# One expert of a top-k mixture computed densely during the routing, the other seven gathered, and the second product turned around

## The reference, cut to what matters

```python
scores = softmax(xt @ Wr)                 # (4096 tokens, 8 experts)
G, idx = top_k(scores.T, 1024)            # each expert picks 1024 tokens
X_in = xt[idx]
h   = gelu(einsum('ekd,edh->ekh', X_in, W1) + b1[:, None, :])   # 128 -> 512
X_e = einsum('ekh,ehd->ekd', h, W2) + b2[:, None, :]            # 512 -> 128
out = zeros((4096, 128)).at[idx].add(G[..., None] * X_e)
x = x + gb * out                          # gb: one row of 128 per batch of 512 tokens
```

## Time and profile before

| | |
|---|---|
| median of 3 runs | 1061.13 us |
| profiled execution | 1051.98 us, its span 1050.2 us |
| mean granted PE clock | 0.858 |
| busy: PE, DVE, POOL, ACT | 822, 581, 453, 433 us |

### The profile page before, as it was taken

The page is one execution under the profiler, slowest core; times in us unless marked ns, Lnnn a source line. Parts: engine busy times, 40 slices in busy tenths (PEclk is TensorE's granted clock), DMA queues, the critical chain, the costliest instruction groups (busy, mean ns, idle before and its releaser), DMA issues. The chain is left out here.

```text
span 1050.2 us, 16881 instructions
## 1 busy us (share of the span) xinstructions
PE 821.7 (78%) x6185; PEld 432.6 (41%) x6185; DVE 580.8 (55%) x1417; ACT 432.5 (41%) x683; POOL 453.2 (43%) x569
## 2 busy tenths in 40 slices
PE   4579898999999999832328999989624999999884
PEld 3223333333334333221215666657412455555443
DVE  3666676757666674116672343300025688888761
ACT  1004554545454455700003233220164687777651
POOL 7201021422323222340026888886546477774423
PEclk9758999989899998955558999985856899999996
DMA  4220443243231311210002333333210100110100
GB/s 125 55 65 10 104 130 82 78 136 86 49 91 42 93 46 46 65 34 11 1 16 48 42 45 42 45 44 29 23 32 10 33 22 12 32 32 22 32 12 20
DMA packets 69289, 50.94 MB, mean 48 GB/s; under 512 B 20241, under 2 KB 63257, under 8 KB 68634
## 3 DMA queue, kind: packets, MB, share of 16 engines
q1 hardware_dynamic: 57946, 41.23, 15.6%
q0 software_dynamic: 11264, 8.66, 6.2%
HBM read 30.78 MB, written 16.99 MB: 45 GB/s over the span
## 5 line engine op out<-in xcount | busy, mean ns | idle before, releaser
L639 DVE TENSOR_REDUCE MX<-bank 128x1 f32<-128x512 f32 (+3 forms) x352 | 215.7, 638 | 87.9 <-PE bank L389 84.0
L503 ACT ACTIVATE PR<-ps_s 128x1024 f32<-128x1024 f32 x160 | 159.0, 1023 | 153.8 <-PE ps_s L353 88.7
L386 PE MATMUL bank<-K,Q 96*128 96x512 bf16 (+3 forms) x512 | 134.6, 323 | 34.5 <-DVE MX L639 18.0
L1043 POOL DMA_INDIRECT d_acc<-Y,idx x64 | 100.1, 1564 | 34.3 <-issue 18.3
L386 PEld LDWEIGHTS bank<-K,Q 96*128 96x128 bf16 x512 | 44.4, 102 | 154.6 <-DVE MX L639 113.3
L1033 POOL DMA_INDIRECT XG<-d_tab,idx x64 | 61.6, 963 | 89.0 <-DVE idx L1158 70.1
L344 PE MATMUL ps_s<-Q,K 99*128 99x512 bf16 x320 | 97.8, 394 | 1.4 <-DMA Q<-d_m 1.3
L1308 ACT ACTIVATE H<-ps_h,b1T 128x512 f32<-128x512 f32 x64 | 44.0, 687 | 122.7 <-PE ps_h L1244 121.3
L389 PE MATMUL bank<-maskT,identb 128*128 128x128 bf16 (+2 forms) x352 | 91.4, 260 | 0.0
L369 PE MATMUL bank<-PR,VE 128*32 128x512 f32 x640 | 90.1, 636 | 0.2 <-ACT PR L503 0.2
L1179 DVE TENSOR_TENSOR Y<-ps_o,XG 128x512 f32<-128x512 f32 x16 | 11.1, 692 | 130.5 <-PE ps_o L1258 122.9
(11 more groups left out here) (282 smaller groups left out, 1407.8 us busy)
## 6 DMA issues: line engine op xcount, KB each, us to landing
Q<-d_q SPq DMA_DIRECT2D x24, 384.0 KB
d_q<-qs SPq DMA_DIRECT2D x24, 128.0 KB, 2.3
d_y<-ysb SPq DMA_DIRECT2D x128, 18.0 KB
d_tab<-tab SPq DMA_DIRECT2D x8, 272.0 KB, 2.4
X<-L_attn_x SPq DMA_DIRECT2D x8, 256.0 KB, 4.9
w<-L_ffn_W SPq DMA_DIRECT2D x8, 256.0 KB, 3.2
d_acc<-zrow SPq DMA_DIRECT2D x1, 2048.0 KB, 9.4
yt<-d_y SPq DMA_DIRECT2D x8, 256.0 KB, 3.3
```

The lines of the kernel that those rows point to most:

```text
L386: nc.tensor.matmul(ps_mx[G % 2][:, x * w:(x + 1) * w], Q[b % QB][0:KR, h, P * g:P * g + P], K[b % QB][0:KR, 0:w], start=(x == 0), stop=Fal ...
L503: nc.scalar.activation(PR[t % 2][:, 2 * half:2 * half + 2, :], ps_s[half][:, :].rearrange("p (a f) -> p a f", a=2), ACT.Exp, scale=DH ** - ...
L639: nc.vector.tensor_reduce(MX[b % 2][:, c:c + len(hs)], ps_mx[G % 2][:, 0:len(hs) * w].rearrange("p (x w) -> p x w", w=w), AX_X, ALU.max).t ...
L1043: nc.gpsimd.indirect_dma_start(out=g.d_acc, out_offset=bass.IndirectOffsetOnAxis(ap=idx[:, e, k:k + 1], axis=0), in_=Y[e % 2][:, k, :], in ...
```

## The change

Expert 0 is taken out of the gathered ones. Its two products are computed for all 4096 tokens, in four chunks of 1024, from plain loads of `d_tab` (XD, the first two share the buffers Y). The chunks 0 to 2 are cut into 56 steps (`dense(k)`) that stand between the routing products of PE; chunk 3 is iteration 8. ITS lists the eleven iterations; the loop over iterations starts at the fourth. ACT writes a chunk's outputs times gb, features on partitions, to YD. After the loop PE transposes YD (L1291) and DVE adds it to X with the selected scores of expert 0 (gate0, zero where not selected).

The seven others (rx is the expert's number less one) keep gather and scatter. `second` now holds w2 and streams 512 columns of H: 8 products of 512 columns instead of 32 of 128 and 8 for the bias. Its result has features on partitions; ACT adds b2 while it copies it to OT (L1414), and PE transposes it back into the same bank (`outputs_T`, L1284) before DVE multiplies. Four lists are made before the loop instead of two, XG has four buffers instead of three, and POOL gathers three experts ahead. Six load semaphores are joined into one, and the chain semaphores are shared between phases.

```diff
+    ITS = (0, 0, 0, 1, 2, 3, 4, 5, 0, 6, 7)
+    LOOP = 3
+    AHEAD = 4
-        gathers(0)
-        gathers(1)
-        for e in range(NE):
-            if e + 2 < NE:
-                gathers(e + 2)
-            scatters(e)
+        for rx in range(3):
+            gathers(rx)
+        for rx in range(NR):
+            if rx + 3 < NR:
+                gathers(rx + 3)
+            scatters(rx)
...
+        for c in range(len(CHUNK_OF)):
             for h in range(2):
+                dve.wait_ge(oT_ps, 2 * NR + 2 * c + h + 1)
+                for i in range(4):
+                    t = NS * c + 4 * h + i
+                    last = V.scalar_tensor_tensor(g.X[:, t, :], ps_o[h][:, P * i:P * i + P], gate0[:, t:t + 1], g.X[:, t, :],
+                                                  ALU.mult, ALU.add)
...
-                for k in range(4):
-                    for c in range(NC_DI):
-                        last = T_.matmul(ps_o[h][:, P * k:P * k + P], H[h][:, c, P * k:P * k + P], g.w2[:, e, c, :],
-                                         start=(c == 0), stop=False)
-                    last = T_.matmul(ps_o[h][:, P * k:P * k + P], ones[0:1, :], B2[0:1, e, :], start=False, stop=True)
+            last = T_.matmul(ps_o[h][:, :], g.w2[:, ITS[it], c, :], H[h][:, c, :], start=(c == 0), stop=(c == NC_DI - 1))
...
+        for r in range(DIGITS):
+            if r >= 2:
+                dense(2 * r - 4)
+                dense(2 * r - 3)
+            pe.wait_ge(cnt_rdy, r + 1)
+            T_.matmul(ps_r[:, 0:3], group[:, :], cnt[:, :], start=True, stop=True).then_inc(sum_rdy, 1)
...
+        for it in range(LOOP, len(ITS)):
+            e, j = ITS[it], it - LOOP
+            for h in range(2):
+                for c in range(NC_DI):
+                    if ITS[it - 1] and h == 0 and c == 2:
+                        outputs_T(it - 1, 1)
+                    first(it, h, c)
...
+            sp.dma_start(XD[c][:, :, :], g.d_tab[CAP * c:CAP * c + CAP, 0:D].rearrange("(k p) f -> p k f", p=P)
+                         ).then_inc(d_in[c], 16)
```

More of the change, by code:

```diff
@@ L244, in program @@
     lgr = sb0("lgr", [P, NT])
[L247 removed]
+    s_x = [sem("x_loaded0"), sem("x_loaded1"), sem("x_loaded_rest")]
     s_w, s_wqkv, s_wrest = sem("weights_loaded"), sem("qkv_weights_loaded"), sem("other_weights_loaded")
@@ L935, in moe @@
     NG = P // NE
+    NR = NE - 1
+    ITS = (0, 0, 0, 1, 2, 3, 4, 5, 0, 6, 7)
+    CHUNK_OF = {it: c for c, it in enumerate(it for it, e in enumerate(ITS) if e == 0)}
+    IT_OF = [ITS.index(rx + 1) for rx in range(NR)]
+    LOOP = 3
+    AHEAD = 4
     GATE = 2 * NS
@@ L1261, in mix_weights_T, with dense @@
+        def dense(k):
+            if k < 2:
+                rows_T(0, k)
+                return
+            it, x = divmod(k - 2, 18)
+            if x in (4, 9):
+                if it + 1 < LOOP:
+                    rows_T(it + 1, x // 9)
+            elif x < 9:
+                u = x if x < 4 else x - 1
+                first(it, u // NC_DI, u % NC_DI)
+            else:
+                second(it, (x - 10) // NC_DI, (x - 10) % NC_DI)
         def mix_weights_T():
-            pe.wait_ge(l_free, 2)
+            pe.wait_ge(l_free, AHEAD)
@@ new lines, in _ @@
+        pe.wait_ge(gt_rdy, 1)
+        T_.matmul(ps_r[:, 256:512], ones[:, :], flat(gt), start=True, stop=True).then_inc(gt_ps, 1)
+        pe.wait_ge(gb_cp, 1)
+        pe.wait_ge(eq_rdy, 1)
+        T_.matmul(ps_l[:, 0:256], upper[:, :], flat(eq), start=True, stop=True)
+        T_.matmul(ps_l[:, 256:512], ones[:, :], flat(eq), start=True, stop=True).then_inc(eq_ps, 1)
+        for k in range(27, 30):
+            dense(k)
+        pe.wait_ge(sel_rdy, 1)
+        T_.matmul(ps_x[1][:, 0:256], upper[:, :], flat(sel), start=True, stop=True)
@@ L1276, in _ @@
+        T_.matmul(ps_x[1][:, 256:512], ones[:, :], flat(sel), start=True, stop=True).then_inc(sel_ps, 1)
+        T_.matmul(ps_r[:, 0:P], ones[:, :], upper[:, :], start=True, stop=True).then_inc(io_ps, 1)
+        for k in range(30, 39):
+            dense(k)
         lists(0)
+        for k in range(39, 45):
+            dense(k)
         lists(1)
-        mix_weights_T()
-        rows_T(0)
-        for e in range(NE):
-            first(e)
-            if e + 2 < NE:
-                lists(e + 2)
-            if e + 1 < NE:
-                rows_T(e + 1)
-            gates(e)
-            second(e)
+        for k in range(45, 51):
+            dense(k)
@@ new lines, in _ @@
+        lists(2)
+        for k in range(51, 56):
+            dense(k)
+        lists(3)
+        mix_weights_T()
+        for h in range(2):
+            rows_T(LOOP, h)
+        for it in range(LOOP, len(ITS)):
+            e, j = ITS[it], it - LOOP
+            for h in range(2):
+                for c in range(NC_DI):
+                    if ITS[it - 1] and h == 0 and c == 2:
+                        outputs_T(it - 1, 1)
+                    first(it, h, c)
+            if e and e - 1 + AHEAD < NR:
+                lists(e - 1 + AHEAD)
+            if it + 1 < len(ITS):
+                for h in range(2):
+                    rows_T(it + 1, h)
+            gates(j)
+            for h in range(2):
+                for c in range(NC_DI):
+                    second(it, h, c)
+            if e:
+                outputs_T(it, 0)
@@ L1288, in _ @@
+        outputs_T(len(ITS) - 1, 1)
+        for c in range(len(CHUNK_OF)):
+            for h in range(2):
+                dense_outputs_T(c, h)
         barrier(pe, 2)
```

307 lines of the change are left out of this document (182 added, 125 removed).

## The result

The changed kernel takes 1031.97 us (median of 4 runs, 1030.56 to 1033.36) against 1060.87 us beside it: ratio 0.973, 95% interval 0.9709 to 0.9752. The forecast of 1029 us missed it by 3 us. The profiled execution took 1031.0 us.

A forecast was written before the change was run, and what follows sets the result against it. Routing was taken as bound by DVE steps, the loop by PE with POOL next; the terms ended the phase 32.9 us earlier, giving 1028 against the median of 1061.13, stated as 1029 us, range 1020 to 1051 (its own range 1021 to 1040).

The forecast's parts named there:

- the sum: Whole expert phase: all terms together end it at 735.9 instead of 768.8, 32.9 us less.
- The term 0 for the rounds: Routing rounds and selection: three slow rounds (+4) offset by later savings, together 0, between -4 and +18 us.
- The 1 us for each of three list stages: Lists ahead of the loop: 1 us lost at each of three, for gaps after which the clock may fall.
- Lists every 7.2 us: Ahead of the loop: each list takes 7.2 us, so the fourth index is ready at 563.9.
- first of the loop near 566 to 569: Loop start: sign of being right, `first` starting there; forecast 568.7 instead of 555.28.
- wrong sign: Signs against: 4 us rounds, lists over 7.5 us apart, a 0.50 stretch in the loop, POOL waiting for Y late there.
- `second` 6.9 us: Loop: 8 products of 512 columns, two passes of 0.43 us each, 6.9 us where `second` took 12.01.
- The 1.5 us waits for R: Loop: PE waits for DVE's R before the list product, 1.5 us in two iterations.
- rival 3: Loop: the low clock reaches into it after PE's waits; one iteration at low clock gives 1070 us; chance 0.07.
- 141.1 us: POOL after the first scatter: 7 scatter batches, 3 gather batches, three landing waits; ends at 728.7.
- 7.3 us from the last scatter to block 1: End of the phase: block 1 starts 7.3 us after the last scatter's issue ends, as before.
- Rival 1: Routing and lists: the clock stays low, 1056 us, or swings half the time, 1042 us; chance 0.18.

The follow-up runs named there:

- e1: Changed kernel unaltered, one execution on another chip, without late list copies: 1018.77 us (before there 1048.41).
- e6: Kernel before with only `second` turned around (w2 stationary); eight experts gathered, nothing dense, two lists ahead: 1038.14 us, ratio 0.9804 to before.
- e8: Changed kernel with all 56 dense steps moved out of the routing, behind the fourth list: 1081.12 us.
- e10: Changed kernel with three lists ahead of the loop, the fourth in it, next rows' transposes before the list, gates between halves of `second`: 1024.29 us, ratio 0.967.
- e4: Changed kernel with TensorE waiting after each of the first three list products until VectorE has copied and used it: 1015.57 us, ratio 0.9693.
- e2: Changed kernel with the seventeen dense steps between the list products moved behind the fourth: 1023.58 to 1030.63 us in three runs, ratio 0.9784.
- e7: Kernel before, unaltered, one execution for a second profile of it: 1056.25 us.
- e9: Changed kernel with no gather issued before the fourth list, on a chip with late copies: 1056.72 us.
- e12: On top of e10, half of the first expert's gathers behind the first index cast, half behind the second, the others behind the third: 1025.29 us, ratio 0.967.
- e5: Changed kernel unaltered, on a chip with late list copies: six runs, 1028.34 to 1037.08 us, ratio 0.9772.
- e11: Changed kernel unaltered, on the same chip as e12, with late list copies: 1034.89 us, ratio 0.9757.
- e3: Changed kernel with no gather issued before the fourth list, on the chip without late copies: 1031.18 us.

## Why the prediction was right, point by point

*Where the gain comes from.* Without late releases the phase took 262.3 us (e1) against the 261.1 forecast, and 31.6 us less than before's 293.9; 32.9 was the sum. With them on both sides it is 303.3 - 277.4 = 25.9. The 28.9 us between the medians lie between the two. The parts of this gain were tried by themselves: `second` (e6) and the hidden dense work (e8).

*The routing.* Shown: the dense work fits, 47.7 us of it (e8). The term 0 for the rounds was some 3 us too high: the clock rose at 485 after the few slow rounds assumed, and the first index came 2.7 to 3.1 us earlier than in before. The 1 us for each of three list stages was not there (e1: 7.15, 7.14 and 7.36 apart), and the loop starts 1.7 us behind the fourth index. So without late releases the loop started 6 us early, at 87.8 for 93.9.

*Lists every 7.2 us* failed in the profile of after, by 14 us, and with it "first of the loop near 566 to 569" (571.24, in a span whose phase began 5.9 us early). It was named as a wrong sign, for the clock's sake. The clock did fall between the lists, to 0.50 at 549.2 to 556 and 562.8 to 573, but the late releases and not the clock made the lists late: in e1 the clock falls between the lists as well (0.50 to 0.51 at 536.9 to 540.3 and 550.6 to 554), and they stay 7.15 us apart. Window of e1:

```profile
550.60:554.00 3.40, 3.40 (x5) 1.33 (x4) 3.26 (x7) 0.78 (x1) 2.49 (x4) 0.51 0.19 41
```

Two more of the wrong signs came, a stretch at 0.50 in the loop and POOL waiting for Y late in the loop (below); the sizes were small enough for the sum to hold.

*`second` 6.9 us* holds: the first begins at 582.52, its transposes at 589.49, 6.97 us.

*Iterations.* Seven of them took 132.0 us in e1 where 127.0 were forecast. The 1.5 us waits for R are there (PE L1241, 1.45 and 1.44 us in after). What was not counted is the clock behind them, as in the earlier trace rows: 22.8 instead of 19.9 us, twice. The prediction had taken it up only in rival 3, and argued that no stop as long as 3.4 us was left; a stop of 1.44 us was enough. e10 speaks for it by taking the wait away. But the fall does not always come: the iterations with the same wait and no fall, one in e4 and two in e2, took 19.5 us. The others came out at 17.8, 17.0, 18.1, 16.6 and 16.8, against 17.8, 17.4, 18.4, 16.8 and 16.8. One reading behind the sum was a little off: of the 17 us by which the loop of before exceeded eight times 22.4, 2.0 lie in its first iteration (24.4 us, the clock at 0.50 up to 560), and not all of them come from the late gather.

*POOL.* 141.1 us were forecast from the first scatter to the end of the last. It was 145.9 in e1 and 142.4 in e4; in this stretch POOL waited for Y 10.7 and 7.1 us, and the longest of these waits, 8.0 and 4.6 us, came before the last scatter batch but one. So PE, by way of Y, and not POOL set the end, though the forecast had both meet. The last scatter sets the end of the phase in all, and the dense sums ended near 731, under the scatters, at no cost.

*7.3 us from the last scatter to block 1* became 9.7. Timeline of after (answers to the earlier trace rows):

```profile
735.40 1.56 POOL L1063 DMA_INDIRECT d_acc<-Y,idx  x1 [0.30 <-issue]
...
746.62 0.36 SPq L1973 DMA_DIRECT2D AC<-d_acc  x1
```

It is 11.1 to 11.3 us from issue to load in every kernel with the dense expert, and 8.7 to 8.8 in those without (e6, e7), so neither chip nor `second` does it. The trace has POOL's drain (its closing instruction in the phase, L1022 in after and L1006 in before) at 7.40 us in after and 4.95 in before. Why it is longer after fewer DMAs stays open; it wasn't tried.

*The clock rule.* The swinging that "TensorE: Matmul & The Clock Gate" (section "A second HAM failure mode: psum-queue depth-cycling") of the Trainium skill warns of did not come in the rounds: with gaps in every round, 32.74 of 40 us busy, the clock stayed at 1.00. Rival 1 falls for the rounds. Between the lists the clock did swing, also in e1, and there it cost 0.2 us at most (casts 7.15, 7.14 and 7.36 us apart). In the loop it cost 3.3 us each time.

*The margin.* That the miss is only 3 us is partly luck. The early start of the loop (-6) is balanced by the clock in the loop (+5) and the drain (+2.4): these are in e1. The late releases were in no term; by the profiles they add 15.1 to after and 9.4 to before. That the median of before, 9 us above its profiled execution, already held them is argued, not shown: no profile of before beside it has them. For it speaks that before took 1048.41 us on the chip without late copies and 1057.8 to 1060.87 on the four others. If so, what before lost to late releases stood in the median that the forecast was made from, unseen.

## What to carry to other kernels

Filling a chain of short steps with independent matrix work cost this chain nothing, since the clock rose with it; the 56 steps put there hid 47.7 us and made the chain 2.7 us shorter. Count on the second bound: turning `second` around saves some 4 us per expert on PE (12.0 us against 7.0 and 1.1 of transposes), and POOL's queue decided what came of it. Where one engine hands short results to another while a third issues indirect DMAs, place the DMAs in the time in which nothing is handed over, and look at a second chip before trusting a step's length.

## What the runs showed of the hardware

- On four of five chips semaphore releases by TensorE arrived late in every profile of the changed kernel and its variants, and on the one of these chips where before was profiled again (e7), in before too: 4.5 to 5.1 us behind the product for a list of the first profile, 4.3 us for a Y in e7's loop, 7.2 us for a list in e10's loop. Ahead of the loop it happened only while POOL's gathers were in flight (e9, e12); in after, e5, e7, e10 and e11 the release came 1.1 to 1.7 us after the issue of the batch's last gather ended. In the loop it happened among scatters as well.
- In e9, on such a chip, TensorE's own instructions were held up too: busy 2.98 of 20 us beside a row of gathers, one list released 20.3 us behind its product. In e3, the same code and the same gathers on the fifth chip, it was busy 10.10 of 10.10 us. What makes a chip so, and by what path gathers hold TensorE up, stays open.
- A wait of some 1.45 us can be enough for TensorE's clock to fall: in e1 to 0.50 or so for 6.8 us (0.64 and 0.51 in two windows of 4 us), though it was busy 3.86 and 4.00 of 4 us. It fell after 17 of the 20 waits of 1.44 to 1.65 us for R in the loops of all profiles; after both in e2 and one in e4 it did not. In the rounds of after, shorter gaps in every round left it at 1.00 from 485 to 530.
- POOL's closing drain took 7.40 us in every profile of a kernel with 112 indirect DMAs and 4.95 in the three with 128 (before, e6, e7). The cause was not tried.
